# Expert gates spread by DMA in place of matmuls, in a fused MoE, adapter and GRU kernel

## What is computed

```
# L0: shared expert plus top-2 of 8 experts, router bias by sequence
shared = (silu(x @ sw1.T) * (x @ sw3.T)) @ sw2.T
s = sigmoid(x @ router_w.T + cond @ router_t_w.T)
idx = top_k(s + router_bias, 2);  gates = s[idx] / (sum(s[idx]) + EPS)
combine = sum(gates * one_hot(idx))                    # (tokens, 8)
x = x + (shared + sum_e combine[:, e] * (gelu(x @ rw1[e].T) @ rw2[e].T)) / 3
# L1: a Haar transform whose bands get one gate and go back: x = x + x * (1 + gate(cond))
# L2: low-rank adapter whose weights come from cond (w = gelu(LN(cond) @ W1) @ W2)
mid = gelu(x @ base_down + (x @ a2) @ b2.T)
x = x + x + mid @ base_up.T + (mid @ b1) @ a1.T
# L3: GRU over the 512 tokens
Z = sigmoid(xz + H @ Whz.T);  R = sigmoid(xr + H @ Whr.T)
H = Z * H + (1 - Z) * tanh(xh + (R * H) @ Whh.T);  Y = H @ Whq.T + bhq
x = x + Y
```

## Time and profile before

| | |
|---|---|
| median of three executions | 1326.75 us |
| the profiled execution | 1327.0 us |
| its span, first to last instruction | 1324.9 us |
| PE busy | 96% of the span |
| PE weight loads busy | 93% |
| DVE busy | 72% |
| ACT busy | 29% |
| GpSimd busy | 9% |
| granted TensorE clock, mean | 0.969 of full |

### The profile page before, as it was taken

The page is one execution under the profiler, slowest core; times in us unless marked ns, Lnnn a source line. Parts: engine busy times, 40 slices in busy tenths (PEclk is TensorE's granted clock), DMA queues, the critical chain, the costliest instruction groups (busy, mean ns, idle before and its releaser), DMA issues.

```text
span 1324.9 us, 53882 instructions
## 1 busy us (share of the span) xinstructions
PE 1278.3 (96%) x22768; PEld 1226.7 (93%) x22768; DVE 949.5 (72%) x6173; ACT 389.7 (29%) x1734; POOL 119.8 (9%) x120
## 2 busy tenths in 40 slices
PE   6989999999999999999999999999999999999965
PEld 6389999999999999999999999999999999999864
DVE  3437777777777777777777777777777777777655
ACT  1013333333333333332333333333333332333222
POOL 2410000000000000000000000000000000000000
PEclk9999999999999999999999999999999999999855
DMA  9400000000000000000000000000000000000000
GB/s 358 136 7 3 10 11 11 11 11 10 4 10 11 11 11 11 11 7 7 11 10 11 11 11 10 7 7 11 11 11 10 11 7 7 11 10 7 7 6 6
DMA packets 8818, 27.84 MB, mean 21 GB/s; under 512 B 2920, under 2 KB 3376, under 8 KB 7296
## 3 DMA queue, kind: packets, MB, share of 16 engines
q1 hardware_dynamic: 5280, 15.41, 3.1%
q0 software_dynamic: 3296, 8.98, 2.1%
HBM read 19.94 MB, written 4.19 MB: 18 GB/s over the span
## 4 chain that ended last, share of the span: by engine, by line
PE 91%; DVE 5%; ACT 1%; DMA 1%; SPq 1%; issue 1%; POOL 0%; DVEq 0%; POOLq 0%
PE bank L363 52%; PE gate_rh L363 29%; PE gate_z L363 10%; DMA own<-in_own 1%; ACT rg L696 1%; DVE x L849 1%; DVE rhp L928 1%; DVE zm L938 0%; DVE zsum L933 0%; ACT zg L696 0%; DVE state L945 0%; DVE rh L929 0%; DVE zh L940 0%; SPq L276 0%; DVE fresh L943 0%
## 5 line engine op out<-in xcount | busy, mean ns | idle before, releaser
L363 PEld LDWEIGHTS gate_rh<-state,whp 128*128 128x128 f16 x6144 | 231.0, 97 | 27.4 <-DVE state L945 19.8
L363 PE MATMUL gate_rh<-state,whp 128*128 128x8 f16 x6144 | 235.4, 167 | 17.7 <-DVE state L945 17.7
L363 PEld LDWEIGHTS gate_rh<-rhp,whp 128*128 128x128 f16 x6144 | 230.4, 97 | 21.2 <-DVE rhp L928 15.0
L696 ACT ACTIVATE rg<-gate_rh 128x16 f32<-128x16 f32 x512 | 93.8, 183 | 519.9 <-PE gate_rh L363 519.9
L363 PE MATMUL gate_rh<-rhp,whp 128*128 128x8 f16 x6144 | 239.4, 167 | 7.5 <-DVE rhp L928 7.5
L928 DVE SCALAR_TENSOR_TENSOR rhp<-rg,hist 128x16 f16<-128x16 f32 x512 | 89.0, 174 | 180.9 <-ACT rg L696 178.7
L696 ACT ACTIVATE zg<-zsum 128x16 f32<-128x16 f32 x512 | 110.6, 216 | 227.4 <-DVE zsum L933 227.4
L363 PE MATMUL gate_z<-state,whp 128*128 128x16 f16 x4096 | 176.6, 169 | 0.0
L938 DVE TENSOR_SCALAR zm<-zg,sscale 128x16 f32<-128x16 f32 x512 | 125.7, 245 | 56.8 <-ACT zg L696 47.5
L363 PE MATMUL bank<-xt,rw 128*128 128x128 f32 x1024 | 160.2, 291 | 6.0 <-DVE sa L829 4.4
L363 PE MATMUL bank<-xt,sw 128*128 128x128 f32 x1024 | 153.4, 290 | 0.0
(11 more groups left out here) (150 smaller groups left out, 1801.8 us busy)
## 6 DMA issues: line engine op xcount, KB each, us to landing
aw<-in_aw SPq DMA_DIRECT2D x4, 2048.0 KB, 19.6
xt<-in_xT POOLq DMA_DIRECT2D x32, 128.0 KB, 2.6
out<-osb POOLq DMA_DIRECT2D x32, 128.0 KB, 2.1
rw<-in_rw SPq DMA_DIRECT2D x2, 1024.0 KB, 11.0
sw<-in_sw SPq DMA_DIRECT2D x3, 512.0 KB, 7.8
wh<-in_wh SPq DMA_DIRECT2D x3, 256.0 KB, 9.4
wx<-in_wx SPq DMA_DIRECT2D x3, 256.0 KB, 18.7
l1w<-in_l1w POOLq DMA_DIRECT2D x2, 256.0 KB, 4.3
```

Of the source, the lines that this page charges most:

```text
L363: return pe.matmul(o, w, x, start=start, stop=stop, skip_group_check=True)
L696: return act.activation(o, i, f, **kw)
```

## The change

The matmuls of `spread_gates` and their semaphores are gone. In their place SP, once `comb` of a block is written, copies it to an 8x128 float32 tensor in DRAM, transposed (elements of 4 bytes), waits until this has landed and until the last products of the block before are made, and copies the 4 KB from there to every partition of a new tile `gates` (512 KB in all). DVE multiplies by `gates`. For block 0 the two transfers stand on SP's queue behind all weight loads and ahead of the copies into `low`; those of the others behind these copies.

The router runs one block further ahead: in block b it is block b+3's (`has_router`), so that `scores` of block 2 and its gate operations join the start. Most of the fill changes its step: `y_out` goes from step 1 to 0, `mid_base` from 0 to 1, all of L2 one step later, the shared expert earlier; the three products of 512 columns on DVE are cut into halves in steps 8 to 13; and `l0_out` is laid anew over steps 11 to 15.

```diff
+            def spread_gates(r):
+                sp.wait_ge(gating, GATE_OPS * (r + 1))
+                if r > 0:
+                    sp.wait_ge(gates_in, 16 * r)
+                sp.dma_start(gates_dram.rearrange("e t -> t e"), comb[:],
+                             allow_slow_non_contiguous=True).then_inc(comb_out, 16)
+                sp.wait_ge(comb_out, 16 * (r + 1))
+                if r > 0:
+                    sp.wait_ge(ge47_done, r)
+                    sp.wait_ge(ge03_done, r)
+                sp.dma_start(gates[:].rearrange("p g c -> p (g c)"),
+                             gates_dram.rearrange("e t -> (e t)").partition_broadcast(P)).then_inc(gates_in, 16)
+
+            spread_gates(0)
             for at, i in enumerate(LOW_ORDER):
                 sp.wait_ge(wrow_dve, 4 * (at + 1))
...
+            for r in range(1, BLOCKS):
+                spread_gates(r)
@@ GpSimd
-                if has_l0:
-                    exp_scores(later(m, 2))
                 if has_y:
                     store(later(m, -1))
+                if has_router:
+                    exp_scores(later(m, 3))
@@ PE, between_z_h: step and what stands in it
-                    if s == 0:
-                        scores(m2, par)
-                    if s == 11:
-                        spread_gates(m2, E47, (4, 5), cb47_done, False)
-                    if s == 12:
-                        spread_gates(m2, A3, (2, 3), cb03_done, True)
+                    if s == 11:
+                        pe.wait_ge(gs_done, count(m2, 1))
+                        l0_out(0, "s", (0, 1), start=True)
+                    if s == 12:
+                        l0_out(1, "s", (1, 2))
+                if has_router and s == 4:
+                    scores(later(m, 3), 1 - par)
@@ PE, between_steps
-                    if s == 0:
+                    if s == 1:
                         mid_base(m1)
-                if has_y and s == 1:
+                if has_y and s == 0:
                     y_out(later(m, -1), q)
-                    if s == 15:
-                        l0_out(0, "r", (2, 3))
-                        l0_out(1, "r", (0, 1, 2, 3), done=l0_done)
+                    if s == 15:
+                        l0_out(1, "r", (2, 3), done=l0_done)
@@ PE, l0_whole_b
-                pe.wait_ge(pe47_done, count(m, 1))
-                spread_gates(m, E47, (4, 5, 6, 7), cb47_done, True)
                 pe.wait_ge(gs_done, count(m, 1))
-                spread_gates(m, A3, (0, 1, 2, 3), cb03_done, True)
@@ PE, the start
             l0_whole_a((0, 1), 1)
+            pe.wait_ge(pe47_done, 2)
+            scores((0, 2), 0)
@@ DVE, gate_op
                 if k == 12:
+                    if m[1] > 0:
+                        dve.wait_ge(comb_out, 16 * m[1])
@@ DVE
-            def times_gate(m, group, p_, ready, mine, done):
-                dve.wait_ge(ready, count(m, 1))
+            def times_gate(m, group, mine, done):
                 dve.wait_ge(mine, count(m, 1))
-                dve.tensor_tensor(ge[:, group], pe_e[:, group], p_[:, :], ALU.mult).then_inc(done, 1)
+                dve.wait_ge(gates_in, 16 * (m[1] + 1))
+                dve.tensor_tensor(ge[:, group], pe_e[:, group], gates[:, group], ALU.mult).then_inc(done, 1)
@@ DVE, early and late
+                    if s == 5:
+                        silu_a1(m2)
+                    if s in (8, 9):
+                        times_a3_part(m2, s - 8)
+                    if s in (10, 11):
+                        times_gate_part(m2, 1, s - 10, pe47_done, ge47_done)
+                    if s in (12, 13):
+                        times_gate_part(m2, 0, s - 12, pe03_done, ge03_done)
+                if has_router:
                     if s == 6:
-                        silu_a1(m2)
+                        add_router_bias(m3)
+                    for at, k in ((11, 4), (14, 8), (14, 9), (15, 10)):
+                        if s == at:
+                            gate_op(m3, k)
+                    for at, k in ((7, 0), (8, 1), (9, 2), (10, 3), (11, 5), (12, 6), (13, 7), (15, 11), (15, 12)):
@@ DVE, the start
             l0_whole_a(m1)
+            add_router_bias((0, 2))
+            gates_whole((0, 2))
             for i in LOW_ORDER:
                 dve.wait_ge(low_in[i], B * 16)
```

More of the change, by code:

```diff
@@ L138, in build @@
         ge = sb("ge", [P, 2, 4 * TOK])
+        gates = sb("gates", [P, 2, 4 * TOK])
         x1 = sb("x1", [P, KC, TOK])
@@ L205, in build @@
         bits_set = sem("bits_set")
+        comb_out = sem("comb_out")
+        gates_in = sem("gates_in")
         biases = sem("biases")
@@ L341, in _, with body @@
             exp_scores((0, 1))
-            def body(m, par, has_y, has_l23, has_l0):
+            exp_scores((0, 2))
+            def body(m, par, has_y, has_l23, has_l0, has_router):
                 if has_l0 and not (type(m[0]) is int and m[1] + 3 >= BLOCKS):
@@ L379, in up_chunks @@
                     i.then_inc(done, 1)
-            def spread_gates(m, ps_, experts, done, last):
-                pe.wait_ge(gating, count(m, GATE_OPS))
-                for e in experts:
-                    i = mm(ps_[:, e % 4 * TOK:(e % 4 + 1) * TOK], comb[:, e:e + 1].to_broadcast([P, P]), ident[:],
-                           True, True)
-                if last:
-                    i.then_inc(done, 1)
             def l0_out(half, kind, chunks, start=False, done=None):
-                for c in chunks:
+                for n, c in enumerate(chunks):
                     w = sw2 if kind == "s" else rw2
                     g = gs[:, c * TOK:(c + 1) * TOK] if kind == "s" else ge[:, c // 4, c % 4 * TOK:(c % 4 + 1) * TOK]
-                    i = mm(l0_ps[:, half], w[:, c, half * P:(half + 1) * P], g, start and c == chunks[0], False)
+                    i = mm(l0_ps[:, half], w[:, c, half * P:(half + 1) * P], g, start and n == 0, False)
                 if done is not None:
@@ L834, in times_a3, with times_a3_part, times_gate_part @@
                 dve.tensor_tensor(gs[:], sa[:], A3[:, :], ALU.mult).then_inc(gs_done, 1)
-            def times_gate(m, group, p_, ready, mine, done):
-                dve.wait_ge(ready, count(m, 1))
-                dve.wait_ge(mine, count(m, 1))
-                dve.tensor_tensor(ge[:, group], pe_e[:, group], p_[:, :], ALU.mult).then_inc(done, 1)
+            def times_a3_part(m, part):
+                columns = slice(part * 2 * TOK, (part + 1) * 2 * TOK)
+                if part == 0:
+                    dve.wait_ge(a3_done, count(m, 1))
+                    dve.wait_ge(sa_done, count(m, 1))
+                i = dve.tensor_tensor(gs[:, columns], sa[:, columns], A3[:, columns], ALU.mult)
+                if part == 1:
+                    i.then_inc(gs_done, 1)
+            def times_gate(m, group, mine, done):
+                dve.wait_ge(mine, count(m, 1))
+                dve.wait_ge(gates_in, 16 * (m[1] + 1))
+                dve.tensor_tensor(ge[:, group], pe_e[:, group], gates[:, group], ALU.mult).then_inc(done, 1)
+            def times_gate_part(m, group, part, mine, done):
+                columns = slice(part * 2 * TOK, (part + 1) * 2 * TOK)
+                if part == 0:
+                    dve.wait_ge(mine, count(m, 1))
+                    dve.wait_ge(gates_in, 16 * (m[1] + 1))
+                i = dve.tensor_tensor(ge[:, group, columns], pe_e[:, group, columns], gates[:, group, columns], ALU.mult)
+                if part == 1:
+                    i.then_inc(done, 1)
             def finish_l0(m, par):
```

142 lines of the change are left out of this document (62 added, 80 removed).

## The result

The changed kernel takes 1591.13 us (median of four executions, 1571.15 to 1595.73) against 1326.11 for the one before on the same chip. Two of the four lie over 1.5% above the fastest, and the ratio is that of the other two (1571.15 and 1586.83): 1.1905 times as long, 95% interval 1.1821 to 1.1989. The profiled execution took 1586.8, 252 us more than the 1334.5 forecast.

A forecast was written before the change was run, and what follows sets the result against it. The prediction took the 2.31 us latency chain of each recurrence step as the bound. Start +31.3, body -24.6 and end +0.75 summed to +7.45 us, giving 1334.5 us, range 1324.0 to 1343.0.

The forecast's parts named there:

- The bound: Recurrence steps: the chain PE, ACT, DVE, PE, ACT, DVE takes 2.31 us; fill is hidden if it fits the gaps.
- The body's new layout: Body: delays in steps 0, 6, 9 and 15 shrink; full block 37.35 us, 0.82 less; 24.6 us gained in all.
- What hides the DMAs: Body: gates needed over 24 us after comb is written, x load has over 8 us; transfers cost nothing.
- Rival (e): Body: 4-byte writes so slow that gates misses step 10, from about 21 us; 1470 at 25 us; chance 0.08.
- The start: Before the first rg: gates of block 0 +22.1, router +6.5, comb's matmuls -1.8, clock +4.5; +31.3 us in all.
- Gates of block 0: Start: transfers queue behind the weight loads, gates land at 56.1, the adapter starts 22.1 us later.
- Router of block 2: Start: scores and gate operations for block 2 stand ahead of the addition to low, which starts 6.5 us later.
- comb's matmuls gone and the clock: Start: 16 records of block 1's comb go, -1.8 us; PE's clock falls after standing idle, +4.5.

The follow-up runs named there:

- contig_strided: Changed kernel with comb written to DRAM untransposed, as 32-byte rows, and VectorE regrouping through a strided read of gates: 1331.66 us, ratio 1.0046.
- start_pe: contig_strided with block 0's gates made by PE as before and comb in two buffers; block 2's router still ahead of the recurrence: 1310.42 us, ratio 0.9873.
- padded_before: Kernel before plus one unused write of comb per block, each 4-byte run on its own 64 bytes of DRAM: 1327.0 us.
- sbuf_before: Kernel before plus one unused copy of comb per block as 1024 4-byte runs into SBUF, 8 bytes apart: 1327.3 us.
- four_a_line: Kernel before plus one unused write of comb per block in 4-byte runs, 4 of them to 64 bytes of DRAM: 1328.4 us.
- own_line_before: Kernel before plus one unused write of comb per block in 4-byte runs, each token's 8 runs sharing 64 bytes of DRAM: 1330.2 us.
- before_scatter: Kernel before plus one unused transposed 4-byte write of comb to DRAM per block from the third on, 16 runs to 64 bytes: 1514.5 us.
- half_before: before_scatter with half of the experts: 512 4-byte runs per block, still 16 to 64 bytes: 1482.8 us.
- tail_scatter: Kernel before plus four unused transposed writes of comb in blocks 30 and 31, where PE has no fill: 1333.6 us.

## Why the prediction was wrong

The direction was right, the size was not: 1334.5 forecast, range 1324 to 1343, 1591 measured. Of the 252 us between forecast and profiled execution, the start has 5, blocks 1 to 29 have 245 (1327.7 measured, 1106.6 - 23.8 = 1082.8 forecast), blocks 0 and 30 have 3.

**The bound: right.** The 2.31 us chain holds. Steps 11 to 14 even came to 2.28, so my floor was 0.03 too high in light steps.

**The body's new layout: right.** By the forecast blocks 1 to 29 lose 24.6 less block 0's 0.8, or 23.8 us; contig_strided, the layout without the small runs, has blocks 1 to 29 in 1081.3 against 1106.6 before, 25.3 less. Its medians, step by step: step 15 2.45 (forecast 2.45), step 1 2.45 (2.48), step 0 2.32 (2.35), step 6 2.31.

**"What hides the DMAs", the step that failed.** I counted the time in which `gates` is not needed, found over 24 us, and wrote down nothing. That was right as far as it went: in the body nobody waits for `gates` in any run. But cover by time only answers who waits for the result. While the write was under way, signals of PE, which doesn't take part in it, came late: that took some 5 us a block (steps 1 and 2), and the clock that falls behind the stall took 3 more. The trace of before had no such write, and I bounded its duration (1.9 to 9.9 us; it took 9.5 to 14), but not what it does to others while it lasts. It was an operation without a row, and I gave its side effects a price of nothing without a reason that excludes one.

**Rival (e)**, slow 4-byte writes, came out nearest in time (1470 at 25 us), but by a mechanism that didn't happen: it asked for 21 us and a missed step 10. The write took about half of that, and no engine waits for a DMA in any block, the x load included.

**The start: +31.3 forecast, +36.1 measured.** Gates of block 0: landing forecast at 56.1, the products start at 56.45; the adapter starts at 63.81 instead of 39.88, +23.9 (forecast 22.1), above all because nearly all 32 records ran at half clock and not 16 (granted clock 0.55 from 57.19 to 63.81): 6.68 us against my 5.1. Router of block 2: the addition stands at 109.98, so this term is 109.98 - 74.92 - 23.9 = +11.2 (forecast 6.5). The 4.7 are the 4.72 us in which `comb` of block 2 waits for the write of block 1 (97.56 to 109.66, 12.1 us; I had said it is done if it takes under 8). Behind it comb's matmuls gone and the clock make +1.0 (forecast +2.7). start_pe and contig_strided give the two large terms apart: 21.3 and 5.1.

That contig_strided ends at 1331.7, close to the 1334.5, says that the other steps of the sum were sound together, partly by errors that offset each other: its start is 27.5 us longer than before, where the sum has 31.3.

**What stays open.** Every stall is a wait for one of PE's semaphores: of `ht` or `rg`, and in a few blocks of DVE's `zsum` for the Z products. By the records PE goes on starting matmuls behind the ones whose signal is late, so a late signal is shown, and a PE that stops working is not. What holds the signal was not shown. In the changed kernel the view of all waits has, for `ht` alone (us in total, times, longest):

```profile
ACT ht L706 <- remote: 87.9, 23, 5.9
```

The trace also loses records there: of the 480 increments of the write's semaphore it holds all in padded_before and sbuf_before, 478 in four_a_line, 389 in own_line_before, 304 in before_scatter and 216 in half_before. Records of the recurrence's own semaphores go with them, 151 of 7168 in the changed kernel and 106 in before_scatter, and none in the kernel before, padded_before and contig_strided. In block 10 the trace has no semaphore record at all from 578.95 to 584.52, although in that time ACT's `zg` (579.16) released DVE's `zm` (579.41). The Trainium skill, NOTIFIC — the notification-queue block, section 7.1, says that the block which writes such records holds its producers back when its internal queue fills. That fits a PE whose signals come late some time after the crowd of writes begins; why records are lost as well would still have to be explained. It is argued, not shown: every execution here was recorded by the profiler, so none tells whether the stalls, and with them most of the 265 us, would be there without its records. This rival is untested.

## What to carry to other kernels

A DMA can be hidden in time and still cost: before its price is put at nothing, ask what its writes do to others while it is under way, and what the clock does behind a stall. Don't write DRAM in 4-byte runs that crowd into the same 64 bytes; write the rows as they lie and do the regrouping in a strided read that has cover (1.4 us against 9 or more, 1332 against 1591 us in all), and if the layout must be transposed, write it in interleaved parts so that few runs meet in 64 bytes at a time. A transfer put at the end of a queue of weight loads costs what the queue holds (10 us here for 4 KB), so let the first block keep the engine that needs no queue.

## What the runs showed of the hardware

- 4-byte writes that meet in the same 64 bytes of DRAM complete at some 0.3 to 0.45 us each: 3.4, 4.7, 5.8 us to completion for 1, 4 and 8 of them; 1024 lone ones cost 3.4 us, and 2.3 into SBUF.
- While 16 to 64 bytes are being written, signals of PE that are due 3.7 to 7.1 us after issue come 1.0 to 5.7 us late (changed kernel, behind each of the 29 writes of blocks 1 to 29), and with no fill on PE too (tail_scatter, 1.1 to 3.2 us). Two writes of 8, one after the other, leave it at 0.8 and 1.2 us in two of 30 blocks. All this in executions under the profiler.
- The individual packets of these writes show 7 to 9 ns each, nearly all, in the trace of before_scatter and all start within 2.6 us of issue, while the last recorded increment comes at 9.4 (median): the packets' own durations don't tell when a write is complete.
- Behind most stalls the granted clock is at half for 3.4 to 27.3 us, with a median of 13.7 in the changed kernel and 6.8 in before_scatter; the steps there take 3.26 to 3.79 instead of 2.31.
